# The signs of the FFN weights made on POOL and DVE, mixed with the magnitudes, in a Mamba and ternary-FFN block

## What is computed

```python
def _quantize(w):
    gamma = jnp.mean(jnp.abs(w))
    return jnp.clip(jnp.round(w / (gamma + EPS)), -1.0, 1.0)

def _bitlinear(x, w):
    return jnp.matmul(x, _quantize(w).T)

x1 = _bitlinear(x, w1)                 # w1, w2: 1408 x 512
x2 = _bitlinear(x, w2)
hidden = jax.nn.sigmoid(x1) * x2
return _bitlinear(hidden, w3)          # w3: 512 x 1408
...
x = x + mixer(xn, ...) + ffn(xn, w1, w2, w3)
```

## Time and profile before

| | |
|---|---|
| median of 3 runs | 1682.27 us (1680.84 to 1683.37) |
| the profiled execution, its own time | 1682.53 us |
| its span, first to last instruction | 1680.7 us |
| PE busy | 1603.4 us (95%) |
| DVE busy | 1129.3 us (67%) |
| ACT busy | 914.9 us (54%) |
| POOL busy | 483.5 us (29%) |
| mean granted PE clock | 0.983 |
| DMA | 89.72 MB, mean 53 GB/s |

### The profile page before, as it was taken

One profiled execution on the slowest core, in us unless ns is written; L12 is line 12 of the kernel. 1 busy time (PEld: TensorE's weight loads), 2 busy tenths in 40 slices (PEclk: granted clock), 3 DMA queues, 4 the chain that ended last, 5 costly groups with the idle time before them and its releaser, 6 DMA issues.

```text
span 1680.7 us, 25539 instructions
## 1 busy us (share of the span) xinstructions
PE 1603.4 (95%) x9426; PEld 785.1 (47%) x9426; DVE 1129.3 (67%) x1836; ACT 914.9 (54%) x1881; POOL 483.5 (29%) x469
## 2 busy tenths in 40 slices
PE   7768679999999999999999999999999999999999
PEld 3334334445445444444444454454544544444544
DVE  7866876678556875667656876568856686567762
ACT  6776545566364653566444663556636564356641
POOL 4222212143131430334212431323403243033320
PEclk9889979999999999999999999999999999999999
DMA  7164330111001210011101210011100211002100
GB/s 256 54 192 127 117 115 20 46 49 53 26 7 58 61 52 3 26 58 45 51 1 39 57 58 26 7 54 55 43 22 14 58 57 51 0 26 69 56 4 26
DMA packets 49277, 89.72 MB, mean 53 GB/s; under 512 B 6112, under 2 KB 7904, under 8 KB 49152
## 3 DMA queue, kind: packets, MB, share of 16 engines
q1 hardware_dynamic: 49152, 88.08, 16.6%
HBM read 79.41 MB, written 8.65 MB: 52 GB/s over the span
## 4 chain that ended last, share of the span: by engine, by line
PE 77%; DVE 7%; ACT 7%; issue 4%; DMA 2%; POOL 0%; SPq 0%; ACTq 0%; DVEq 0%; POOLq 0%
PE bank L605 18%; PE bank L517 13%; PE bank L621 9%; PE bank L411 9%; PE bank L427 8%; PE bank L584 7%; PE bank L437 4%; ACT edc L846 3%; PE bank L549 2%; PE bank L561 2%; PE bank L534 1%; PE bank L574 1%; DVE edc L1219 1%; DMA full<-w_ffn 1%; DVE mdc L1225 1%
## 5 line engine op out<-in xcount | busy, mean ns | idle before, releaser
L517 PE MATMUL bank<-wx_hi,arena 128*128 128x512 f16 x1024 | 320.5, 383 | 0.0
L605 PE MATMUL bank<-xt_hi,q 128*128 128x512 f16 x704 | 268.1, 381 | 4.3 <-ACT q L913 4.3
L605 PE MATMUL bank<-xt_lo,q 128*128 128x512 f16 x704 | 267.9, 381 | 0.0
L1487 POOL TENSOR_TENSOR xst<-xdt,dst 128x512 f32<-128x512 f32 x64 | 66.7, 1042 | 566.4 <-DVE xdt L1173 566.4
L517 PE MATMUL bank<-wx_lo,arena 128*128 128x512 f16 x512 | 196.3, 383 | 0.0
L621 PE MATMUL bank<-q,arena 128*128 128x512 fp8e4 x704 | 162.4, 379 | 0.0
L846 ACT ACTIVATE edc<-csl,csv 128x128 f32<-128x128 f32 x512 | 155.7, 389 | 1.1 <-DMA csl<-sums 1.1
L517 PEld LDWEIGHTS bank<-wx_hi,arena 128*128 128x128 f16 x1024 | 101.2, 99 | 115.3 <-issue 4.7
L1219 DVE TENSOR_TENSOR edc<-edc,gt 128x512 f32<-128x512 f32 x128 | 87.8, 726 | 67.2 <-ACT edc L851 67.1
L1274 DVE SCALAR_TENSOR_TENSOR full<-tnh,bank 128x512 f32<-128x512 f32 x88 | 60.5, 687 | 103.2 <-PE bank L605 101.6
L879 ACT CAST arena<-full 128x512 f16<-128x512 f32 x88 | 54.6, 620 | 138.1 <-DVE full L1274 138.1
(11 more groups left out here) (207 smaller groups left out, 3526.3 us busy)
## 6 DMA issues: line engine op xcount, KB each, us to landing
csl<-sums SPq DMA_DIRECT2D x128, 256.0 KB, 3.2
full<-w_ffn SPq DMA_DIRECT2D x33, 256.0 KB, 3.1
res<-x SPq DMA_DIRECT2D x32, 256.0 KB, 3.9
out<-res SPq DMA_DIRECT2D x32, 256.0 KB, 2.0
res<-w_ffn SPq DMA_DIRECT2D x24, 256.0 KB, 3.7
yac<-x SPq DMA_DIRECT2D x16, 256.0 KB, 2.7
gate<-x SPq DMA_DIRECT2D x16, 256.0 KB, 3.5
arena<-w_in SPq DMA_DIRECT2D x4, 512.0 KB, 8.4
```

What stands on the lines that cost most here:

```text
L517: i = pe.matmul(banks[0][:], act[:, k, c * P:(c + 1) * P], wt[:, k, hf * half:(hf + 1) * half], start=(n == 1), stop=(n == 3 * ki))
L605: i = pe.matmul(banks[2 * (m % 2) + j][:], q12[:, j, k, m * P:(m + 1) * P], part[:, k, :], start=(n == 1), stop=(n == 2 * kd))
L1487: pool.tensor_tensor(by_head(xst[:], hd), by_head(xdt[:], hd), heads_over(sml["dst"][:, c, :], hf * hph, hph, hd), ALU.mult).then_inc(S["x ...
```

## The change

- A sign tile is now two comparisons: POOL writes `w < -gamma/2` as bytes (`less`, two buffers), DVE writes `(w > gamma/2) - less` straight into the fp8 tile. ACT has no part in it; gamma is not inverted, and DVE keeps the bounds `above` and `under`.
- The sums and bounds are made for each matrix by itself. Signs of w1 start while magnitudes of w2 and w3 are still read.
- The list is written out by hand, two steps at each place of a unit (one at two places of the last). 15 sign tiles lie in the units and 18 beside the FFN, two at each m from 1 to 9. The places in the projections, which were empty, are gone.
- One ring of four (`full0`, `full1`, `raw0`, `raw1`) takes all loads in the units; the ring beside the FFN is `raw0`, `raw1`, `edc0`, `edc1`. `res1` and `res3` are no longer part of a ring.
- w1 and w2 are laid out so that one tile holds one m of the up products (`q12[:, j, m, k, :]`). PE waits for single tiles: tile m of w1 and of w2 before their products, tile m of w3 before the down products.
- POOL now also works off the list: one place before `scan`, two behind it, one after `project_x` of the next unit; beside the FFN nine places, and `root` of the next block behind the fifth.

```diff
-BESIDE_PROJ = [0, 0, 0]
-BESIDE_UNIT = [[3, 3, 3, 3], [3, 3, 3, 3], [3, 3, 3, 3], [2, 2, 2, 1],
-               [2, 1, 2, 1], [2, 1, 2, 1], [2, 1, 2, 1], [2, 2, 2, 1]]
+BESIDE_UNIT = [[2, 2, 2, 2]] * 7 + [[2, 1, 1, 2]]
-    prep = [("mag", n) for n in range(12)] + [("wout", k) for k in range(ki)]
-    prep += [("mag", n) for n in range(12, n_ff)] + [("sums", 0), ("scales", 0)]
-    prep += [("tern", n) for n in range(n_ff - beside_ffn)] + [("end", 0)]
-    prep += [("tern", n) for n in range(n_ff - beside_ffn, n_ff)] + [("end", 0)]
+            kind = {"M": "mag", "O": "wout", "S": "sums", "B": "scales", "T": "tern"}[kind]
...
+    prep = list(kinds("M M M M M M M M  M M M O S O O O  O O O O M B M M  T M T M T M M M  T M T M T M T S "
+                      "M T M B T M M T  M T M T M M M M  M T S T B T " + "T T " * beside_ffn))
...
-        early_ring = [full[0], full[1], res[1], res[3]]
-        late_ring = [full[0], full[1], res[3]]
-        ffn_ring = [edc[0], edc[1], xs[0], xs[1]]
+        raw_flat = [r[:].rearrange("p b t -> p (b t)")[:, 0:half] for r in raw]
+        ring = [full[0][:], full[1][:], *raw_flat]
+        ffn_ring = [*raw_flat, edc[0][:], edc[1][:]]
...
 SP, load_prep
+                if kind == "tern" and n >= n_early:
+                    use = n - n_early
+                    if use >= 4:
+                        sp.wait_ge(S["tern_q"], n - 3)
+                    elif use >= 2:
+                        sp.wait_ge(S["m_lo"], at(0, "m_lo", 12 + use))
                     else:
+                        sp.wait_ge(S["tern_q"], n_early)
+                        sp.wait_ge(S["mag"], n_ff)
...
 PE, ffn_up and ffn_down
-                        pe.wait_ge(S["gam"], 1)
+                        pe.wait_ge(S["gam"], 3)
+                    if b == 0:
+                        pe.wait_ge(S["tern_q"], j * pieces_per + m + 1)
-                            i = pe.matmul(banks[2 * (m % 2) + j][:], q12[:, j, k, m * P:(m + 1) * P],
+                            i = pe.matmul(banks[2 * (m % 2) + j][:], q12[:, j, m, k, :],
+                        if c == b == 0:
+                            pe.wait_ge(S["tern_q"], 2 * pieces_per + m + 1)
-                if b == 0:
-                    pe.wait_ge(S["tern_q"], 2 * pieces_per)
-                if b == 0:
-                    pe.wait_ge(S["tern_q"], n_ff)
...
 ACT, prep_second
-                    act.wait_ge(S["tern_b"], n + 1)
-                    act.wait_ge(S["wx_lo"], halves * ki)
-                    act.activation(q_flat[j][:, i * half:(i + 1) * half], buf[:], ACT.Copy,
-                                   bias=-ROUND, saturate=False).then_inc(S["tern_q"], 1)
...
 DVE, prep_first and prep_second
-                    dve.tensor_scalar(buf[:], buf[:], rgam[:, j:j + 1], ROUND,
-                                      ALU.mult, ALU.add).then_inc(S["tern_a"], 1)
-                    dve.wait_ge(S["tern_a"], n + 1)
-                    dve.tensor_scalar(buf[:], buf[:], ROUND + 1.0, ROUND - 1.0,
-                                      ALU.min, ALU.max).then_inc(S["tern_b"], 1)
+                    dve.wait_ge(S["gam"], n + 1)
+                    dve.tensor_scalar(above[:, n:n + 1], gam[:, n:n + 1], 0.5, None, ALU.mult).then_inc(
+                        S["bounds"], 1)
+                    dve.tensor_scalar(under[:, n:n + 1], gam[:, n:n + 1], -0.5, None, ALU.mult).then_inc(
+                        S["bounds"], 1)
+                    dve.wait_ge(S["bounds"], 2 * (j + 1))
+                    dve.wait_ge(S["below"], n + 1)
+                    dve.scalar_tensor_tensor(out=signs(n), in0=place, scalar=above[:, j:j + 1],
+                                             in1=less[n % 2][:], op0=ALU.is_gt,
+                                             op1=ALU.subtract, saturate=False).then_inc(S["tern_q"], 1)
...
 POOL, prep
+                    pool.wait_ge(sem, landed)
+                    pool.wait_ge(S["bounds"], 2 * (j + 1))
+                    if n >= 2:
+                        pool.wait_ge(S["tern_q"], n - 1)
+                    pool.tensor_scalar(less[n % 2][:], place, under[:, j:j + 1], None, ALU.is_lt).then_inc(
+                        S["below"], 1)
```

More of the change, by code:

```diff
@@ L1 @@
+from collections import Counter
 from contextlib import ExitStack
@@ L111, in mamba_ffn_block @@
               *(f"z_in{n}" for n in range(4)), "bc_in", *(f"wx_in{n}" for n in range(8)),
-              *(f"early{n}" for n in range(4)), *(f"late{n}" for n in range(3)),
+              *(f"early{n}" for n in range(4)),
               *(f"beside{n}" for n in range(4)), "sums_out", "sums_in0", "sums_in1")}
@@ L188, in mamba_ffn_block @@
         asum = sb("asum", [P, 3, pieces_per])
-        tsum, gam, rgam = (sb(n, [P, 3]) for n in ("tsum", "gam", "rgam"))
+        tsum, gam, above, under = (sb(n, [P, 3]) for n in ("tsum", "gam", "above", "under"))
+        less = [sb(f"less{n}", [P, half], mybir.dt.uint8) for n in range(2)]
         wx_stage = [t[:] for t in res] + wx_later
@@ L226, in prep_cuts, with signs, landing @@
             left = list(prep)
-            for n in (*BESIDE_PROJ, *(n for unit in BESIDE_UNIT for n in unit), *[1] * (kf - 1)):
+            for n in (*(n for unit in BESIDE_UNIT for n in unit), *[2] * beside_ffn):
                 yield [left.pop(0) for _ in range(n)]
+        def signs(n):
+            j, m = divmod(n, pieces_per)
+            return q3[:, m, :] if j == 2 else q12[:, j, m].rearrange("p k n -> p (k n)")
+        def landing(kind, n):
+            if kind == "tern" and n >= n_early:
+                s, landed = slot(4, n - n_early)
+                return ffn_ring[s], D[f"beside{s}"], landed
+            s, landed = slot(4, loaded.index((kind, n)))
+            return ring[s], D[f"early{s}"], landed
         def sync_program(sp):
@@ L242, in load_prep @@
             def load_prep(kind, n):
[L243 to L250, removed]
-                    else:
-                        was, m = early[use - 4]
+                if kind not in ("mag", "wout", "tern"):
+                    return
@@ L950, in scalar_program @@
                 cuts = prep_cuts()
-                before = [("end", 0)]
                 def aside():
@@ L1419, in vector_program @@
                     split_state(b, u)
+                if b == 0:
+                    prep_second(*before[0])
+                    before[0] = ("end", 0)
                 for m in range(kf):
@@ L1471, in x_branch @@
                     pool.wait_ge(S["cleared"], 7)
+                if b == 1 and m == 0:
+                    pool.wait_ge(S["tern_q"], n_ff)
                 pool.tensor_copy(r[:, :, 0:halo], hal[:, m, :, :]).then_inc(S["halo_in"], 1)
@@ L1526, in gpsimd_program @@
                     before_chunk(b, u)
+                    aside()
                     scan(b, u)
+                    aside()
+                    aside()
                     if u + 1 < len(units):
                         project_x(b, u + 1)
+                    aside()
+                for m in range(1, beside_ffn + 1):
+                    aside()
+                    if m == 5 and b < nb - 1:
+                        root(b + 1)
                 if b < nb - 1:
-                    root(b + 1)
                     for m in range(ki):
@@ L1573 @@
         "w_out": np.ascontiguousarray(get("L0_attn_out_proj_w").T),
-        "w_ffn": np.concatenate([tiles(get(f"L0_ffn_w{n}")) for n in (1, 2, 3)], axis=1),
+        "w_ffn": np.concatenate([tiles_by_row(get("L0_ffn_w1")), tiles_by_row(get("L0_ffn_w2")),
+                                 tiles(get("L0_ffn_w3"))], axis=1),
         "ident": np.eye(P, dtype=np.float32),
```

169 lines of the change are left out of this document (73 added, 96 removed).

## The result

The changed kernel takes 1663.95 us (median of four, 1663.38 to 1666.29) beside 1682.35 us of the kernel before on the same chip: a ratio of 0.9897, 95% interval 0.9885 to 0.991. That is 18.4 us faster. The forecast was 1644 us, 38 us faster, with a range of 1630 to 1662: the direction and the place are right, the size is half, and the time lies outside the range. The profiled execution took 1663.81 us for a span of 1662.0.

What follows compares the result with a forecast made beforehand. Tensor engine bounds the kernel, 95% busy, idle mostly in block 0. Units 92.7 + 7.5 = 100.2 us, then 3.3 to the FFN: start 186.5 instead of 224.25, 37.8 earlier; forecast 1644 us, range 1630 to 1662.

Steps and rivals of the forecast that it cites:

- Where the time can be had: Block 0, first product of unit 0 to first FFN product: at most 55.2 us can be had, only there.
- Who sets the pace: Units 0 to 6 in block 0: larger of ACT's and PE's sums, taken by pairs of units, 92.7 us.
- The allowance of 7.5 us: Added to the units' 92.7 us: landings 4, slots held by sign tiles 2, POOL collisions 1.5.
- Landings and the ring: Loads in the units: 4 us for landings, 2 for held slots, worst in unit 6; ACT's waits at most 8.
- The first rival: Ring in units 2 to 6: an ACT wait like 2.59 us in each, 13 us, time 1656; chance 0.17.
- POOL's comparison: New POOL operation per sign tile: 1.04 us, ends 0.19 and 1.49; collisions in the units cost 1.5 us.
- It fits with 0.16 us to spare: Beside the FFN: DVE needs 3.29 us of a 3.45 us step; with some 4.5 us slack for hid_f, no loss.
- the second rival: DVE bounds the FFN: 18 operations each lose 0.94 us to POOL, 11 us after slack, time 1655; chance 0.09.
- The clock at the FFN start: First FFN products' low clock may vanish, up to 2.1 us; flag reads may cost as much; taken as 0.
- the fifth: Rival: FFN products wait for tern_q after all, up to 4.29 us, time 1649, inside the range; no separate chance.
- Full overlap: Rival: ACT's sum or the tensor engine's alone sets the pace, plus the clock, 1627 to 1634; chance 0.09.
- the slower one: Rival: POOL's comparison far above its neighbours; all gain gone at 3.6 us, each us beyond costs 33; chance 0.04.

Runs made afterwards that it cites:

- the three hindrances: Removed from the changed kernel together: four-buffer ring (now five), late w_out, DVE's fourth place before the residual sum; 1653.10 us with POOL's comparison, 1656.53 with both on DVE.
- the fastest version: Changed kernel with five buffers, w_out early, DVE's fourth place late, both comparisons on DVE in units, old three-operation signs beside the FFN: 1648.91 us.
- the mended list: Changed kernel with w_out tiles earlier, w1's sum and bounds spaced apart, one sign tile moved from unit 3 to unit 6: 1661.38 us, ratio 0.988.
- the fifth buffer: Changed kernel with res3 added to the ring of the units, five buffers instead of four: 1659.90 us, ratio 0.9867.
- the repaired one: Changed kernel's list with five buffers, w_out early and DVE's fourth place late: 1653.10 us with POOL's comparison, 1656.53 with both comparisons on DVE.
- the short comparison: Changed kernel with POOL's comparison on one of 512 columns, nearly all signs of -1 left out: 1657.87 us, ratio 0.9857.
- three repairs: Changed kernel with fifth ring buffer, mended w_out order and DVE's late fourth place, each alone 1659.90, 1661.38 and 1663.32 us; together, POOL's comparison kept, 1653.10.

## Why the prediction was wrong, step by step

**Where the time can be had.** Right: only block 0 changed, and the two parts of the account (21.7 and -2.9 us) close it to 0.1 us.

**Who sets the pace: the step that failed.** "It may lag by a unit and catch up, so I take the larger of the two by pairs." By the pairs the units should have taken 92.7 us; they took 117.3. The allowance of 7.5 us on top covers less than a third of the 24.6 between. The rule treats ACT and PE as two queues that run side by side and meet only at the larger sum. The runs say otherwise, twice. With 13.6 us of ACT's work left out, 3.1 us were gained. With the three hindrances of this list gone and POOL out of the units, they still take 105.6 us (the fastest version). Inside a unit the engines work in series: PE's transposition waits for DVE's residual sum, the output projection for yt_lo and wo_lo, DVE's sums for ACT's copies, and each of these stands behind a place of the list. A late release is paid by PE at once, as in unit 6 (timelines of ACT, DVE and PE, changed kernel):

```profile
193.27 0.63 ACT L900 ACTIVATE full<-full 128x512 f32<-128x512 f32 x1 [3.22 <-DMA full<-w_ffn]
...
194.51 0.69 DVE L1158 TENSOR_TENSOR xdt<-xs,dt 128x512 f32<-128x512 f32 x1 [2.08 <-ACT xs L816]
...
198.25 0.68 DVE L1250 SCALAR_TENSOR_TENSOR res<-bank,res 128x512 f32<-128x512 f32 x1
...
198.98 1.11 PE L579 MATMUL bank<-idn,yac 128*128 128x128 f32 x4 [6.25 <-DVE res L1250]
```

A magnitude at the third place waits for its landing, so ACT makes `xs` late, DVE makes `xdt` late, and the residual sum, whose products PE had ended by 192.1, comes behind them in DVE's order. PE waits 6.25 us. A lag isn't caught up in the next unit either, since PE has its full work there too. The larger of the two, taken for each unit, would have given 14.2 + 13.6 + 16.1 + 12.4 + 15.4 + 11.8 + 13.0 = 96.5, only 3.8 more; the sums were the wrong tool, not only the pairing. The view that would have said so was at hand: PE's own waits in the units, 18.3 us for `res`. The prediction goes by ACT's waits and leaves PE's out.

**The moved w_out: a step not priced at all.** The prediction counts w_out steps among ACT's, unit by unit, and never asks when PE first wants them. The last low part lies at the third place of unit 2, and the first output projection is in unit 2. PE waits 5.6 us, then runs ten products at half the clock. This is the main cause of the long unit 2, shown by the mended list (16.3 us). What the repair is worth at the end is only 2.5 us by itself.

**Landings and the ring.** About right. The prediction's worst case, unit 6's third place, is there: ACT waits 3.2 us. All of ACT's waits come to 11.8 us, above the 8 given as a limit, and the fifth buffer gives 3.6 us, where 4 + 2 were allowed. The first rival (1656, a wait of that kind in each of units 2 to 6, 13 us) had the sum of the waits about right, and their price wrong: they are only partly on the path. The longest is on it, as unit 6 above shows.

**POOL's comparison.** Too short: 1.56 us at least, above my upper end of 1.49. In the units its length costs 2.3 us with this list, where 1.5 were allowed. Against both comparisons on DVE it costs 1.0 us with this list and 0.6 with the repaired one.

**Beside the FFN.** "It fits with 0.16 us to spare" failed, at a small price. The sum was made for DVE alone; its second sign operation waits for POOL and is then 0.4 us longer, in nearly every second step, and the root of the next block costs one long step. The slack that the prediction counts, for hid_f two steps later, did hold. What it had not asked is when PE wants the next block's tokens, which stand in the same queue of DVE: PE waits 3.0 us for them. The stretch is 2.9 us longer than before, the second rival in kind (it had 11 us), and the short comparison takes 4.0 us off it. Against DVE's sum: with both comparisons on DVE a step takes 4.27 us.

The page "SBUF — State Buffer" of the Trainium skill (section "SBUF: two separate sides") says that a two-input DVE operation and a GpSimd one exclude each other on a shared port pair. The trace agrees only in part: DVE's operation takes 1.15 us instead of 0.74 where it starts 0.1 us behind the start of a comparison (223.90), and POOL's goes from 1.56 to 1.90 where it starts while such an operation of DVE runs (220.36, 228.04). But the loser does not wait to the other's end: DVE's ends at 225.05, POOL's at 225.38, and at 222.88 the same DVE operation takes its 0.74 us in the middle of a comparison that runs from 222.24 to 223.8. The prediction's own row on this, DVE's 1.37 us, is an operation with one SBUF input, so it doesn't bear the two-input rule out.

**The clock at the FFN start.** Taken at no gain; in fact the first products are 0.21 us apart, where before 4.15 us ran at a clock of 0.52, some 2 us. So nearly the 2.1 us named as a bound were gained here, and some 1.7 lost again behind the wait at L399. The low clock doesn't hang on the wait for the signs, though. PE is at half clock in unit 7 in the changed kernel too, after the wait of 6.25 us (timeline of PE), and gets the full clock back only just before the FFN:

```profile
201.19 0.61 PE L566 MATMUL bank<-xst_hi,arena 128*128 128x512 f16 x1
```

With the short comparison the FFN starts without a wait for signs as well, and its first 2 us still have a clock of 0.61. Whether the low clock reaches into the FFN differs from run to run, and the runs don't show what decides it. So two stretches can differ by up to some 2 us for the clock alone.

**The other rivals.** No FFN product waits for its signs: the fifth is out. Full overlap (1627 to 1634) is out, and so is the slower one: the comparison is far from 3.6 us.

**What stays open.** The fastest version's units sum to 105.6 us. With its list, the larger of PE's own step and ACT's sum, taken for each unit, is 14.2 + 14.2 + 16.1 + 12.4 + 15.4 + 11.8 + 12.8 = 96.9, 8.7 us less. PE is idle for 16.1 us there: 5.3 for `res`, 2.9 for `yac`, 6.3 before the scan, the rest in small waits. The 6.3 are again `xdt_lo` (DVE's and PE's timelines, fastest version; the operation ends at 108.81):

```profile
107.84 0.97 DVE L1182 SCALAR_TENSOR_TENSOR xdt_lo<-xdt,xdt_hi 128x512 f16<-128x512 f32 x1 [0.70 <-ACT xdt_hi L829]
...
108.91 0.21 PE L561 MATMUL bank<-xdt_hi,mdc 128*128 128x64 f16 x1 [2.20 <-issue]
```

So the largest part of PE's idle time is the end of one chain: PE's projection, ACT's `xs`, DVE's `xdt`, ACT's `xdt_hi`, DVE's `xdt_lo`, the scan. A third engine's sum is missing as well. The prediction gives DVE idle time in every unit, but with both comparisons DVE is busy for 15.36 us of unit 4's 16.33 and 14.94 of unit 6's 15.91; with DVE as the third the larger sums come to 99.4. In the changed kernel DVE has more room (14.79 of 19.15 in unit 4). How the last 6.2 us divide over the links was not tested by a run.

## What to carry to other kernels

When a change moves steps in a list that several engines work off, look up for each moved step who uses its result first, and put the two moments beside each other, before adding up any engine's time. Read the waits of the engine that bounds the kernel before those of the engine that seems to feed it, and don't let two engines' sums stand for a unit in which they release each other. Waits hide each other: three repairs worth 6.8 us one by one gave 11.4 together, so a repair that gives nothing alone isn't refuted; and each stage may want its own way of doing the same work, here two comparisons on DVE in the units and three operations without POOL beside the FFN.

## What the runs showed of the hardware that I had not expected

- A POOL comparison of 128 x 512 floats into bytes takes 1.56 us, longer than POOL's two-input operations of the same size at 1.04 to 1.49; on DVE it takes 0.48.
- On one column the same POOL operation still takes about 0.6 us at the median, and 0.28 to 1.2 in all (by tile, the run with the short comparison):

```profile
L1508 POOL TENSOR_SCALAR less<-raw,under x19: 286/621/1197, 129.8 to 243.0; 128x1 uint8<-128x1 f32 x19
```

- DVE's operation with a byte input and an fp8 output takes 0.74 us, against 0.68 for the all-float form and 0.43 for a one-input form in place.
- PE's clock stayed low for ten products (4 us) after a wait of 5.6 us in unit 2. After the wait of 6.25 us that ended at 198.98 it stayed low up to about 202.4, over products that followed without a pause, so a wait in the units can slow the start of the FFN (a clock of 0.61 over its first 2 us with the short comparison, where PE did not wait there).
- A DVE operation with two SBUF inputs can run at its usual length (0.74 us) while a POOL comparison is under way; beside the FFN it is 0.3 us or more longer only where the two start close together.
